# In the last step, the first image is mixed in the convolutions' PSUM banks and the second in the mixing banks

## The reference

```
x1 = relu(conv3x3(x, dilation 2));  x2 = relu(conv(x, x1));  x3, x4 likewise      # dense block, 32 channels each
fea = relu(concat(x, x1, x2, x3, x4))                    # 160 channels
fea = H fea H^T                                          # 2-D DCT of every channel
y   = conv3x3(fea, w6) + b6 + x                          # 160 -> 32 channels
# quantised block, each activation and weight fake-quantised to 4 bits by its largest magnitude:
z = relu(conv1x1(q(y)));  z = relu(depthwise3x3(q(z)));  out = conv1x1(q(z)) + y
```

## Time and profile before

| | |
|---|---|
| median of three runs | 437.0 us |
| profiled execution, its own time | 435.09 us |
| its span | 433.3 us |
| PE busy | 375.0 us (87%) |
| DVE busy | 298.9 us (69%) |
| ACT busy | 232.4 us (54%) |
| mean granted PE clock, share of full | 0.941 |

### The profile page before, as it was taken

The page is one execution under the profiler, slowest core; times in us unless marked ns, Lnnn a source line. Parts: engine busy times, 40 slices in busy tenths (PEclk is TensorE's granted clock), DMA queues, the critical chain, the costliest instruction groups (busy, mean ns, idle before and its releaser), DMA issues. The chain is left out here.

```text
span 433.3 us, 7852 instructions
## 1 busy us (share of the span) xinstructions
PE 375.0 (87%) x2770; PEld 264.6 (61%) x2772; DVE 298.9 (69%) x552; ACT 232.4 (54%) x378; POOL 18.0 (4%) x18
## 2 busy tenths in 40 slices
PE   4886998999999999999999999999294473799696
PEld 3563687686777868778786876877093121455332
DVE  5546645848874885796588478568736899477856
ACT  6133563753665475376467537526444695177640
POOL 3000000000000000000000000000000700022000
PEclk9996999999999999999999999999778599699959
DMA  8445225333622433353242242334000000000004
GB/s 257 106 142 162 52 47 121 106 84 73 162 62 58 113 92 84 85 152 81 65 114 71 73 107 74 85 73 96 2 2 0 2 0 0 0 3 2 3 26 169
DMA packets 19533, 32.56 MB, mean 75 GB/s; under 512 B 4528, under 2 KB 11568, under 8 KB 19504
## 3 DMA queue, kind: packets, MB, share of 16 engines
q1 hardware_dynamic: 19504, 32.17, 28.6%
HBM read 11.38 MB, written 2.10 MB: 31 GB/s over the span
## 5 line engine op out<-in xcount | busy, mean ns | idle before, releaser
L649 PE MATMUL sums_ps<-D,w_hl 128*128 128x512 f32 x576 | 147.8, 414 | 13.4 <-DVE D L416 6.0
L649 PEld LDWEIGHTS sums_ps<-D,w_hl 128*128 128x128 f32 x576 | 109.6, 192 | 53.1 <-DMA D<-D 8.6
L327 ACT ACTIVATE Y<-mix_ps 128x288 f32<-128x288 f32 x120 | 48.9, 410 | 37.5 <-PE mix_ps L741 25.3
L737 PE MATMUL mix_ps<-mix_hl,F_hl 128*128 128x288 f32 x360 | 66.7, 304 | 1.5 <-DVE St L449 0.7
L737 PEld LDWEIGHTS mix_ps<-mix_hl,F_hl 128*128 128x128 f32 x360 | 56.5, 195 | 5.1 <-issue 2.5
L287 ACT ACTIVATE r<-sums_ps,bias_sb 64x512 f32<-64x512 f32 x32 | 21.9, 683 | 66.0 <-PE sums_ps L649 65.8
L409 DVE TENSOR_TENSOR r<-mix_ps,r 64x512 f32<-64x512 f32 x16 | 11.1, 693 | 42.6 <-ACT r L295 21.2
L1142 PE MATMUL ps<-q_q,q_diag 64*64 64x512 bf16 x576 | 35.7, 408 | 2.0 <-DVE q_q L1034 2.0
L398 DVE CAST D<-r 64x512 fp32r<-64x512 f32 x48 | 19.8, 411 | 25.0 <-ACT r L287 25.0
L946 ACT ACTIVATE q_I<-ps,w_bias 128x1024 f32 x24 | 25.4, 1110 | 19.9 <-PE ps L1142 19.9
L741 PE MATMUL mix_ps<-mix_hl,X 96*128 96x288 f32 x120 | 35.8, 304 | 0.0
(11 more groups left out here) (118 smaller groups left out, 438.0 us busy)
## 6 DMA issues: line engine op xcount, KB each, us to landing
D<-D SPq DMA_DIRECT2D x96, 126.0 KB, 2.4
F<-r SPq DMA_DIRECT2D x96, 64.0 KB, 2.0
x_own<-in_x_pads SPq DMA_DIRECT2D x16, 288.0 KB, 4.0
F<-in_x_mix SPq DMA_DIRECT2D x16, 128.0 KB, 2.7
xb<-in_x_res SPq DMA_DIRECT2D x8, 256.0 KB, 2.9
out<-q_res SPq DMA_DIRECT2D x8, 256.0 KB, 2.0
w_raw<-in_w_conv SPq DMA_DIRECT2D x6, 192.0 KB, 4.1
w_raw<-in_w_int SPq DMA_DIRECT2D x1, 843.0 KB, 4.7
```

Source lines behind the costliest of these rows:

```text
L327: nc.scalar.activation(Y[:, u, g], banks(p, u)[:, g % 4, 0:MIX], ACT.Copy).then_inc(y_out, 1)
L649: last = nc.tensor.matmul(conv_ps[u][:, bank, :], w_hl[:, wp, n, d, :], D[f][u][:, xp, :, 2 * d:2 * d + S], start=start and d == 0 and h == 0,
L737: nc.tensor.matmul(y, F_hl[u][:, xp, h, k], mix_hl[:, wp], start=n == 0, stop=False, skip_group_check=True)
```

## The change

In the last step the two images of pair 7 swap PSUM halves: `banks` now gives `sums_ps` for image 0 and `mix_ps` for image 1. `stage3` and `turn_back` use `banks(p, u)` too, so image 0's third stage lands in `sums_ps`. The waits follow. Image 0's groups wait only for the convolution sums in their own banks: groups 0 and 1 for `added[0]`, 2 and 3 for `added[1]`. Image 1 waits for pair 6's `turn_s1` and `turn_back`.

The orders of step 8 follow. PE: image 0's whole mix comes first, then the wait and pair 6's two `stage3`, then image 1; its first four groups have all `mix_rows` ahead of the wait for `X4`. DVE: `turn_s1` of pair 6's image 0 moves into step 7, between `low_4(0)` and `low_4(1)`; in step 8 `turn_s1(p, 0)` stands ahead of `largest(p - 1)`, and `turn_s1(p, 1)` behind `add_up(p, 0)` and `largest_last(0)`. ACT: the second copy of X4 becomes a function of its own, `copy_4`; in the last step before the end, image 1's copy moves into step 8, between the first and the last four groups of `take_mix(p, 0)`. No computation is added or removed.

```diff
--- before.py
+++ after.py
@@ -163,7 +163,7 @@
 
         def banks(p, u):
 
-            return sums_ps if u and is_before_last(p) else mix_ps
+            return sums_ps if not u and is_before_last(p) else mix_ps
 
         def is_first(s):
             return isinstance(s, int) and s == 0
@@ -312,17 +312,20 @@
                     k = slice(32 * h, 32 * h + 32)
                     last = nc.scalar.activation(X4[u][k, h], r[u][k].rearrange("p a b l -> p (a b l)"), ACT.Relu)
                 last.then_inc(x4_hi[u], 1)
+
+            def copy_4(u):
+
                 for h in range(2):
                     k = slice(32 * h, 32 * h + 32)
                     last = nc.scalar.activation(X4[u][64:96, h], r[u][k].rearrange("p a b l -> p (a b l)"),
                                                 ACT.Relu)
                 last.then_inc(x4_copied[u], 1)
 
-            def take_mix(p, u):
+            def take_mix(p, u, groups=range(8)):
 
                 n = p * 2 + u
                 act.wait_ge(s1_done, p + GRANT)
-                for g in range(8):
+                for g in groups:
                     act.wait_ge(y_done, n * 8 + g + 1)
                     nc.scalar.activation(Y[:, u, g], banks(p, u)[:, g % 4, 0:MIX], ACT.Copy).then_inc(y_out, 1)
 
@@ -356,7 +359,9 @@
             def step(s, odd, batch):
                 p = s - 1
                 if is_last(s):
-                    take_mix(p, 0)
+                    take_mix(p, 0, range(4))
+                    copy_4(1)
+                    take_mix(p, 0, range(4, 8))
                     take_mix(p, 1)
                     return
                 relu(s, 1, 0)
@@ -378,7 +383,10 @@
                 take_part(s, 4, 0)
                 take_part(s, 4, 1)
                 high_4(s, 0)
+                copy_4(0)
                 high_4(s, 1)
+                if not is_before_last(s):
+                    copy_4(1)
 
             steps(act, step)
 
@@ -448,7 +456,7 @@
                 dve.wait_ge(s3_done, p * 2 + u + (1 + GRANT))
                 nc.vector.transpose(
                     St[:, u].rearrange("p (l i) -> p l i", i=C),
-                    mix_ps[:, 2 + u, 0:PX // 4].rearrange("p (o l) -> p l o", o=C)).then_inc(st_done, 1)
+                    banks(p, u)[:, 2 + u, 0:PX // 4].rearrange("p (o l) -> p l o", o=C)).then_inc(st_done, 1)
 
             def add_up(p, u, odd, batch):
 
@@ -580,18 +588,17 @@
 
                 before = 1 - odd, batch - odd
                 if is_last(s):
-                    turn_s1(p - 1, 0)
                     turn_s1(p - 1, 1)
                     turn_back(p - 1, 0)
                     turn_back(p - 1, 1)
                     add_up(p - 1, 0, *before)
                     add_up(p - 1, 1, *before)
+                    turn_s1(p, 0)
                     largest(p - 1, *before)
-                    turn_s1(p, 0)
                     turn_back(p, 0)
-                    turn_s1(p, 1)
                     add_up(p, 0, odd, batch)
                     largest_last(0)
+                    turn_s1(p, 1)
                     turn_back(p, 1)
                     add_up(p, 1, odd, batch)
                     largest_last(1)
@@ -633,6 +640,8 @@
                 add_parts(s, 4, 0)
                 add_parts(s, 4, 1)
                 low_4(s, 0)
+                if is_before_last(s):
+                    turn_s1(p, 0)
                 low_4(s, 1)
 
             steps(dve, step)
@@ -716,11 +725,8 @@
             def mix_ready(p, u):
 
                 pe.wait_ge(f_lo[u], p + 1)
-                if banks(p, u) is sums_ps:
-                    for v in range(2):
-                        pe.wait_ge(added[v], 2 * PAIRS)
-                else:
-                    for done in (zt_done, st_done) if u or is_before_last(p) else (zt_done,):
+                if banks(p, u) is not sums_ps:
+                    for done in (zt_done, st_done) if u else (zt_done,):
                         pe.wait_ge(done, p * 2 + GRANT)
 
             def mix_x4_ready(p, u):
@@ -732,6 +738,8 @@
                 h, k = g // 4, slice(NP * (g % 4), NP * (g % 4) + NP)
                 if g >= 4:
                     pe.wait_ge(y_out, (p * 2 + u) * 8 + (g - 3))
+                elif banks(p, u) is sums_ps and g % 2 == 0:
+                    pe.wait_ge(added[g // 2], 2 * PAIRS)
                 y = banks(p, u)[:, g % 4, 0:MIX]
                 for n, (wp, xp) in enumerate(((0, 0), (0, 1), (1, 0))):
                     nc.tensor.matmul(y, F_hl[u][:, xp, h, k], mix_hl[:, wp],
@@ -768,7 +776,7 @@
                 pe.wait_ge(zt_done, p * 2 + (u + 1 + GRANT))
                 zt = Zt[:, u, :].rearrange("p (o q l) -> p q o l", q=4, o=C)
                 for q in range(4):
-                    last = nc.tensor.matmul(mix_ps[32 * q:32 * q + 32, 2 + u, 0:PX // 4], hr[:], zt[:, q],
+                    last = nc.tensor.matmul(banks(p, u)[32 * q:32 * q + 32, 2 + u, 0:PX // 4], hr[:], zt[:, q],
                                             start=True, stop=True, skip_group_check=True)
                 last.then_inc(s3_done, 1)
 
@@ -776,9 +784,6 @@
                 p = s - 1
                 dct = not is_first(s)
                 if is_last(s):
-                    pe.wait_ge(zt_done, p * 2 + GRANT)
-                    for u in range(2):
-                        stage3(p - 1, u)
                     mix_ready(p, 0)
                     for g in range(4):
                         mix_rows(p, 0, g)
@@ -788,10 +793,14 @@
                     for g in range(4, 8):
                         mix_rows(p, 0, g)
                         mix_x4(p, 0, g)
+                    pe.wait_ge(zt_done, p * 2 + GRANT)
+                    for u in range(2):
+                        stage3(p - 1, u)
                     mix_ready(p, 1)
+                    for g in range(4):
+                        mix_rows(p, 1, g)
                     mix_x4_ready(p, 1)
                     for g in range(4):
-                        mix_rows(p, 1, g)
                         mix_x4(p, 1, g)
                     stage1(p, 0)
                     for g in range(4, 8):
```

## The result

The changed kernel took **426.9 us** (four runs, 425.96 to 428.07) against 437.0 in the same comparison: ratio 0.9766, 95% interval 0.9735 to 0.9796. Measured once more, in a later comparison, it took 427.81 against 436.7: ratio 0.9789, interval 0.9753 to 0.9825. (Some runs of a kernel took 610 to 721 us; the ratios leave them out.) The prediction was 428.1 us. It put 0.5 on more than 2% and 0.48 on less; the first comparison lies wholly beyond 2%, the second holds 2% in its interval.

What follows compares the result with a forecast made beforehand. The prediction saw no engine as the bound, but one chain of handovers in the tail, with PE idle and its clock halved. 8.3 + 0.6 = 8.9 us off 435.1 gave 426.2, plus 1.9 offset 428.1 us; range 425.9 to 430.7.

Steps and rivals of the forecast that it cites:

- Parts 1 to 3: Step 8: image 0 mixed at once, DVE's turn moved earlier, image 1 following; stage1 of image 0 starts 8.3 us earlier.
- Part 4: End of step 8, stage1 of image 0 to last reduce: the new order gains 0.6 us, bounds 0 to 0.9.
- The sum: Whole kernel: 8.3 from the earlier start plus 0.6 from the end's order, 8.9 us off the profiled 435.1.
- the offset of one execution: Whole kernel: the median stood 1.9 us above the profiled execution, and this was carried into the forecast time.
- The case's own range: Forecast case, 426.3 to 429.8 us: 0.3 either way for wakeups and the end's order, 1 for the clock behind the barrier.
- The first rival: PE's clock falls in the new gaps between 305 and 308.3: 2.1 us lost, 430.2 us; chance 0.2.
- The row set against it: Kernel before, near 330: a 1.34 us hole left PE's clock at full, taken as evidence that it stays up.
- The early stretch: Kernel before, from 31.97: seven matmuls with holes, 1.63 us busy of 3.42, next stretch at half clock; evidence for falling.
- The second rival: Step 8 to the end: PE's clock falls and stays down, 438.3 us, slower than before; chance 0.02.
- The third: Image 1's start is held elsewhere, such as low_4(1) stalling 1 us on DVE: 429.1 us; chance 0.06.

Runs made afterwards that it cites:

- the four variants that kept these holes or shortened them: Changed kernel with DVE's turn back in step 8, DVE's old end, reduce behind the turn, or that plus image 1's X4 later: tails 25.83, 25.33, 24.60, 24.10 us.
- the larger hole of 3.25: Changed kernel plus four unused ACT instructions, 0.63 us each, behind high_4(1), delaying PE's group 4: tail 29.68 us, ratio 0.9899 to the kernel before.

## Why the prediction was right

By its own steps, each counted from the first `stage1` matmul of pair 6 (301.40 before, 302.61 after):

| step | predicted | after |
|---|---|---|
| first mixing matmul | 3.2 | 3.13 |
| group 4 starts | 6.9 | 6.90 |
| second turn ends | 9.1 | 9.09 |
| image 1 starts | 11.0 | 10.97 |
| `stage1` of image 0 starts | 13.2 | 13.26 |
| last reduce ends | 24.7 | 24.92 |

- **Parts 1 to 3** hold in order and size: 21.48 became 13.26, 8.2 against 8.3. The hole ahead of group 4 is ended by ACT's first copy, as said.
- **Part 4** was mis-sized: 12.09 became 11.66, 0.43 and not 0.6. The old order put back cost 0.41. Of the missing 0.17, 0.06 are rounding: the sum's own terms (4.18 to `stage3`, 7.05 of durations, eight handovers of 0.04) make 11.55, not 11.5. Another 0.08 are the two `add_up`, 1.43 each where the sum had 1.39, a row that overlaps others. The handovers make up the rest; the longest, 0.13, is ahead of `add_up` at 321.35.
- **The sum** of 8.9 compares with 8.65 in the first pair of profiles and 8.9 in the mean of the repeated tails. The time of 428.1 was carried over by the offset of one execution; the medians were 426.9 and 427.8. The case's own range of 426.3 to 429.8 is wider than its two terms, 0.3 and 1 each way, which make 426.8 to 429.4; the measured 426.9 is only just inside those.
- **The first rival** did not come about in the changed kernel where it mattered: its holes of 0.34 and 0.69 left the clock at 1.00, in both its profiles and in those of the four variants that kept these holes or shortened them. But it was closer than 0.2 sounds: with ACT's old order the hole is 1.98, the clock fell in both executions, and it cost 1.50 us, near the 1.6 worked out for the case in which it is back at once. The row set against it, a hole of 1.34 near 330, was no test of these places. In the changed kernel even a hole of 1.81, ahead of the last `stage3` at 324.45, left the clock at 1.00 until 326.60. Both of these holes stand behind long dense work, while the 1.98 stand behind only 0.79 us of it and another hole. The early stretch rests on one execution: with the same holes the clock stayed up there in another (last section). The Trainium skill (TensorE: Matmul & The Clock Gate, "A second HAM failure mode: psum-queue depth-cycling") tells of frequent short idles between groups of matmuls that make the clock swing between its levels. The changed kernel, with holes of 0.34, 0.69 and 0.66 within 5.9 us and a clock of 1.00, does not do so. With ACT's old order the clock fell once and came back, though at a hole of 1.98.
- **The second rival,** a clock that stays low to the end, was nowhere to be seen: with the larger hole of 3.25 the clock was back 14.4 us into the tail, with PE's old order and its hole of 5.94 after 14.7. **The third** would have been a start of image 1 past 11.0; it was at 10.97.
- The prediction gave ACT's reorder no price of its own: it placed the first copies ahead of the moved `copy_4(1)` and went on. The expectation for that run put it at a shift of 1.3 us. It also keeps the hole short and so the clock up; its worth is 2.8 us.

## What to carry to other kernels

When the last pass over a buffered pipeline leaves a bank free, ask which engine's queue could use it first, and reorder that queue: everything but PE's order gave 2.2 us here, PE's order with the clock that it keeps up 6.5 more. Then follow the engine that releases the new work, since a copy that comes 1.3 us later cost 2.8 once the hole let the clock fall. And take a tail's gain between two instructions in both traces, since here the rest of the kernel moved by up to 2.5 us ahead of it and 2.4 behind it, in executions with the same work.

## What was not expected of the hardware

- The clock fell with a hole of 1.98 us behind one of 0.33, although PE worked ahead of it, between the holes and behind, in both of two profiles. Holes of 0.34 and 0.69 in the same places never did it in five, nor 0.34 and 0.17 in a sixth. Where between these it turns, and whether 1.3 us in this place would do it, stays open.
- The length of a hole alone does not decide it. In the changed kernel PE stood idle for 1.81 us from 322.63, behind 9.05 us of nearly unbroken work from 313.58, and the clock stayed at 1.00 through the `stage3` that followed.
- The same holes can do either. Early in the kernel before, PE has a hole of 1.68 us, one short matmul group and a hole of 0.87. In its first profile the clock was at half from 35.39 on the earlier trace rows, inside the second of these holes; in its second, with holes of 1.68 and 0.86 at the same place, it stayed at full, also through a hole of 3.23 that followed:

```profile
35.06 0.27 PE L662 MATMUL mix_ps<-ident,stat 128*3 128x128 f32 x1 [1.68 <-DVE stat L503]
...
43.92 3.52 PE L649 MATMUL sums_ps<-D,w_hl 128*128 128x512 f32 x9 [3.23 <-DVE r L411]
```

```profile
33.37:43.92 10.55, 3.72 (x14) 1.00 0.60 161
```

So a clock that stayed up in two profiles of the changed kernel is no promise for each execution. What decides between them is not shown.
